# A mixture-of-experts kernel: tables moved to GpSimd, weight pieces twice as wide, norm sums placed inside a step

## What is computed

```python
def _gemma_mlp(x, gate_w, up_w, down_w):
    g = jnp.einsum('bsh,hi->bsi', x, gate_w)          # 128 -> 512
    u = jnp.einsum('bsh,hi->bsi', x, up_w)
    return jnp.einsum('bsi,ih->bsh', gelu(g) * u, down_w)

rw = jax.nn.softmax(router_logits, axis=-1)           # (32, 8)
w, sel = jax.lax.top_k(rw, 2); w = w / w.sum(axis=-1, keepdims=True)
w = scale * w + (1.0 - scale) * stop_gradient(w)      # scale = 1/12
out = sum over experts e of dense_w[:, e] * _gemma_mlp(x, skill_gate[e], skill_up[e], skill_down[e])
out = out + _gemma_mlp(x, shared_gate, shared_up, shared_down)
return x + out
```

## Time and profile before

| | us |
|---|---|
| median of 3 runs | 214.37 (213.44 to 215.72) |
| the profiled execution, its own time | 213.45 |
| its span on the core | 211.6 |
| TensorE busy | 202.7 |
| ScalarE busy | 137.6 |
| VectorE busy | 127.8 |
| GpSimd busy | 107.9 |

### The profile page before, as it was taken

One profiled execution on the slowest core, in us unless ns is written; L12 is line 12 of the kernel. 1 busy time (PEld: TensorE's weight loads), 2 busy tenths in 40 slices (PEclk: granted clock), 3 DMA queues, 4 the chain that ended last, 5 costly groups with the idle time before them and its releaser, 6 DMA issues.

```text
span 211.6 us, 6607 instructions
## 1 busy us (share of the span) xinstructions
PE 202.7 (96%) x2663; PEld 162.8 (77%) x2663; DVE 127.8 (60%) x231; ACT 137.6 (65%) x225; POOL 107.9 (51%) x110
## 2 busy tenths in 40 slices
PE   7999597999989999999999999999999999999995
PEld 2345353544434468899999999999999999999995
DVE  4796986788889999754434434435435344444451
ACT  6356377799997999656556566565565665655650
POOL 3002324446544666765655656556556556565562
PEclk9999999999999999999999999999999999999999
DMA  6999600000000000000010010010010010010011
GB/s 203 402 427 437 268 3 0 2 3 0 0 0 0 0 3 5 0 5 3 3 50 3 3 52 4 0 53 3 5 51 5 0 53 3 5 50 3 3 53 53
DMA packets 2814, 11.70 MB, mean 55 GB/s; under 512 B 353, under 2 KB 609, under 8 KB 2401
## 3 DMA queue, kind: packets, MB, share of 16 engines
q1 hardware_dynamic: 2640, 11.01, 13.0%
q10 hardware_dynamic: 144, 0.26, 0.5%
HBM read 9.18 MB, written 2.10 MB: 53 GB/s over the span
## 4 chain that ended last, share of the span: by engine, by line
PE 68%; ACT 11%; DVE 3%; issue 1%; DVEq 0%
PE o_ps L670 7%; PE u_ps L650 7%; PE g_ps L650 7%; PE o_ps L668 7%; PE u_ps L652 7%; PE g_ps L652 7%; PE o_ps L669 7%; PE u_ps L651 7%; PE g_ps L651 7%; ACT gel L298 3%; ACT wsk L320 3%; ACT h L303 3%; ACT wsk L315 1%; PE o_ps L631 1%; PE o_ps L632 1%; PE o_ps L633 1%
## 5 line engine op out<-in xcount | busy, mean ns | idle before, releaser
L271 POOL TENSOR_TENSOR h<-h 128x512 f16<-128x512 f32 x92 | 106.1, 1159 | 99.2 <-ACT h L303 68.8
L453 DVE SCALAR_TENSOR_TENSOR h<-gel,sk_factor,u_ps 128x512 f32<-128x512 f32 x64 | 47.8, 747 | 66.5 <-PE u_ps L652 35.3
L298 ACT ACTIVATE gel<-g_ps,sk_gate 128x512 f32<-128x512 f32 x64 | 44.0, 687 | 48.8 <-PE g_ps L652 48.8
L303 ACT CAST h<-h 128x512 f16<-128x512 f32 x92 | 56.4, 613 | 4.9 <-DVE h L453 4.6
L652 PE MATMUL g_ps<-x,wsk 128*128 128x128 f16 x256 | 46.2, 219 | 0.0
L652 PE MATMUL u_ps<-x,wsk 128*128 128x128 f16 x256 | 46.2, 219 | 0.0
L651 PE MATMUL g_ps<-x,wsk 128*128 128x128 f16 x256 | 46.2, 219 | 0.0
L651 PE MATMUL u_ps<-x,wsk 128*128 128x128 f16 x256 | 46.2, 219 | 0.0
L650 PE MATMUL g_ps<-x,wsk 128*128 128x128 f16 x256 | 46.1, 219 | 0.0
L650 PE MATMUL u_ps<-x,wsk 128*128 128x128 f16 x256 | 46.1, 219 | 0.0
L670 PE MATMUL o_ps<-h,wsk 128*128 128x128 f16 x256 | 45.9, 219 | 0.0
(11 more groups left out here) (107 smaller groups left out, 307.2 us busy)
## 6 DMA issues: line engine op xcount, KB each, us to landing
wsk<-skills SPq DMA_DIRECT2D x3, 2048.0 KB, 16.5
outT<-xT SPq DMA_DIRECT2D x7, 256.0 KB, 2.0
xT<-xT SPq DMA_DIRECT2D x2, 768.0 KB, 6.8
wsh<-shared SPq DMA_DIRECT2D x3, 256.0 KB, 3.8
xT<-xT ACTq DMA_DIRECT2D x1, 256.0 KB, 3.4
xT<-xT SPq DMA_DIRECT2D x1, 256.0 KB, 5.2
outT<-xT SPq DMA_DIRECT2D x1, 192.0 KB, 2.8
outT<-xT SPq DMA_DIRECT2D x1, 64.0 KB, 1.6
```

The source lines that it names most:

```text
L271: nc.gpsimd.tensor_tensor(hidden_lo(t), hidden_full(t), hidden_hi(t), ALU.subtract).then_inc(lo_ok, 1)
L298: nc.scalar.activation(gel[:, t % NG, :], g_ps[t % 2][:, :], ACT.Gelu_apprx_tanh, scale=scale).then_inc(gelu_ok, 1)
L303: nc.scalar.copy(hidden_hi(t), hidden_full(t)).then_inc(hi_ok, 1)
L453: nc.vector.scalar_tensor_tensor(out=h32[:, t % N32, :], in0=gel[:, t % NG, :], scalar=factor, in1=u_ps[t % 2][:, :], op0=ALU.mult, op1=AL ...
```

## The change

**Front.** The first four steps take group 0 of x instead of group 7, and the groups follow in their order. ScalarE fetches group 0 and behind it, on the same queue, the router logits, which SyncE fetched first of all before; SyncE so starts with the shared weights. The set FIRST holds x of groups 0 and 1 (`XF = 2`), X_NEXT groups 2 to 4, X_REST groups 5 to 7. `routing_weights` and `routing_spread` move from the front and from step 4 to VectorE's step 3.

**Order.** The maxima of groups 5, 6, 7 move to steps 10, 11, 11, the mask and the sum of X_REST to steps 12 and 13; `routed_tables` from 7 to 11; `add_group(0)` from 10 to 7. The splits of x move to one or two steps earlier relative to their use; that of group 0, needed by the experts only, is new at step 3. On TensorE `spread_norms` stands between d and u of its step rather than behind u. On VectorE `scales` stands ahead of `mask`.

**Tables.** All factor tables are made by GpSimd, between its `hidden_lo`: FIRST ahead of the steps, X_NEXT in step 4, X_REST in step 14, the experts' in step 22. VectorE waits for them where it uses a new one.

**Experts' weights.** The down matrix gets its norm by `gram` on TensorE in steps 15 to 18; ScalarE's `squares` are gone. The experts' weights are split in 6 pieces of 2048 columns, at steps 12, 16, 20, 24, 28 and 32, instead of 12 of 1024 every other step from 12 to 34.

```diff
-        TOP_AT = {1: (1,), 3: (2, 3), 5: (4, 5), 6: (6, 7)}
-        K_STEPS = [5, 9]
-        MASK_AT = {3: X_NEXT, 6: X_REST, 8: K_GATE, 12: K_UP, 22: K_DOWN}
-        SPREAD_AT = {4: X_NEXT, 7: X_REST, 9: K_GATE, 13: K_UP, 23: K_DOWN}
-        SQUARES_AT = {11: 0, 13: 1, 17: 2, 21: 3}
+        TOP_AT = {1: (2,), 3: (3, 4), 10: (5,), 11: (6, 7)}
+        K_STEPS = [5, 10, 15]
+        MASK_AT = {3: X_NEXT, 9: K_GATE, 12: X_REST, 14: K_UP, 19: K_DOWN}
+        SPREAD_AT = {4: X_NEXT, 10: K_GATE, 13: X_REST, 15: K_UP, 20: K_DOWN}
         ROUTE_AT = 6
+        ROUTED_AT = 11
+        TABLE_AT = {4: X_NEXT, 14: X_REST}
+        SKILL_TABLES_AT = 22
-        X_AT = {5: 1, 8: 7, 9: 2, 10: 3, 15: 4, 19: 5, 23: 6}
-        EG = 2
-        PIECES = {12 + 2 * n: n for n in range(3 * E // EG)}
+        X_AT = {3: 0, 5: 2, 8: 3, 10: 4, 14: 5, 18: 6, 22: 7}
+        EG = 4
+        PIECES = {12 + 4 * n: n for n in range(3 * E // EG)}
...
         def _(sp):
-            sp.dma_start(logits[:, :], cond).then_inc(cond_in, 16)
...
         def _(act):
-            act.dma_start(xT32[:, (G - 1) * GN:], xT[:, (G - 1) * GN:]).then_inc(x_in[0], 16)
+            act.dma_start(xT32[:, 0:GN], xT[:, 0:GN]).then_inc(x_in[0], 16)
+            act.dma_start(logits[:, :], cond).then_inc(cond_in, 16)
...
             probabilities()
-            routing_weights()
             for q in (GATE, UP, DOWN):
                 top_shared(q)
             top_x(0)
+            top_x(1)
             mask(FIRST)
...
-                if t in MASK_AT:
-                    mask(MASK_AT[t])
                 if t in SPREAD_AT:
-                    n = SPREAD_AT[t]
-                    scales(n)
-                    if n == X_NEXT:
-                        shared_tables(1, XA, 2)
-                    if n == X_REST:
-                        shared_tables(XA, G, 3)
-                        inverse_table()
-                if t == C:
+                    scales(SPREAD_AT[t])
+                if t in MASK_AT:
+                    mask(MASK_AT[t])
+                if t == C - 1:
+                    routing_weights()
                     routing_spread()
-                if t == ROUTE_AT + 1:
+                if t == ROUTED_AT:
                     routed_tables()
-                if t == 24:
-                    skill_tables()
-
-                if t == 10:
+
+                if t == 7:
                     add_group(0)
...
                     if down_of(t) >= C and down_of(t) != down_of(t - 1):
                         down_shared(down_of(t))
+                    if t in SPREAD_AT:
+                        spread_norms(SPREAD_AT[t])
                     half_shared(t, UP)
...
-                if t in SPREAD_AT:
-                    spread_norms(SPREAD_AT[t])
...
-                for kind in range(2):
+                for kind in range(3):
                     n = t - K_STEPS[kind]
                     if 0 <= n < 4:
...
                 if t in PIECES:
                     pool.wait_ge(sk_lo_ok, PIECES[t] + 1)
                 nc.gpsimd.tensor_tensor(hidden_lo(t), hidden_full(t), hidden_hi(t), ALU.subtract).then_inc(lo_ok, 1)
+                if t in TABLE_AT:
+                    shared_tables(TABLE_AT[t])
+                if t == SKILL_TABLES_AT:
+                    skill_tables()
```

More of the change, by code:

```diff
@@ L46, in build @@
     N32 = 4
+    XF, XA = 2, 5
     NG = 3
@@ L169, in build @@
         stored = sem("stored")
[L174 to L176 removed]
+        FIRST, X_NEXT, K_GATE, X_REST, K_UP, K_DOWN = range(6)
+        K_OF = (K_GATE, K_UP, K_DOWN)
+        COLS = [(DC, XC + XF), (XC + XF, XC + XA), (KC, KC + 1), (XC + XA, XC + G), (KC + 1, KC + 2), (KC + 2, KC + 3)]
         def group(t):
[L181 to L196 removed]
+            return t // C
+        TOP_AT = {1: (2,), 3: (3, 4), 10: (5,), 11: (6, 7)}
+        TOP_OF = {FIRST: 3 + XF, X_NEXT: 3 + XA, X_REST: 3 + G}
+        K_STEPS = [5, 10, 15]
+        MASK_AT = {3: X_NEXT, 9: K_GATE, 12: X_REST, 14: K_UP, 19: K_DOWN}
+        SPREAD_AT = {4: X_NEXT, 10: K_GATE, 13: X_REST, 15: K_UP, 20: K_DOWN}
+        ROUTE_AT = 6
+        ROUTED_AT = 11
+        TABLE_AT = {4: X_NEXT, 14: X_REST}
+        SKILL_TABLES_AT = 22
+        X_AT = {3: 0, 5: 2, 8: 3, 10: 4, 14: 5, 18: 6, 22: 7}
+        X_NTH = {1: 1} | {j: n + 2 for n, j in enumerate(X_AT.values())}
+        EG = 4
+        PIECES = {12 + 4 * n: n for n in range(3 * E // EG)}
         def lag(t):
@@ L305, in x_high @@
             def x_high(j):
-                act.wait_ge(scaled, (FIRST if j == 0 else X_NEXT if j < XA else X_REST) + 1)
+                act.wait_ge(scaled, (FIRST if j < XF else X_NEXT if j < XA else X_REST) + 1)
                 nc.scalar.activation(x_part(j, 0), x_full(j), ACT.Copy, scale=sc[:, XC + j:XC + j + 1]).then_inc(x_hi_ok, 1)
[L309 to L315, removed]
             def skill_high(n):
                 kind, w, hi, _ = piece_of(n)
-                act.wait_ge(scaled, K_GATE + kind + 1)
+                act.wait_ge(scaled, K_OF[kind] + 1)
                 nc.scalar.activation(hi, w, ACT.Copy, scale=sc[:, KC + kind:KC + kind + 1]).then_inc(sk_hi_ok, 1)
@@ L363, in mask @@
                 a, b = COLS[n]
-                if n < K_GATE:
+                if n not in K_OF:
                     dve.wait_ge(top_ok, TOP_OF[n])
                     nc.vector.tensor_tensor(top2[:, a:b], top[:, a:b], top[:, a:b], ALU.mult).then_inc(diag_ok, 1)
[L367 to L370, removed]
-                else:
-                    dve.wait_ge(sq_ok, E // 2)
-                    nc.vector.tensor_scalar(sq_floor[:, :], sq_sum[:, :], NORM_FLOOR, None, ALU.add).then_inc(diag_ok, 1)
+                else:
+                    kind = K_OF.index(n)
+                    dve.wait_ge(gram_ok, kind + 1)
+                    nc.vector.scalar_tensor_tensor(out=diag[:, :], in0=n_ps[0][:, 0:P], scalar=NORM_FLOOR,
+                                                   in1=ident[:, :], op0=ALU.add, op1=ALU.mult).then_inc(diag_ok, 1)
             def scales(n):
@@ L378, in scales @@
                 norm = n_ps[1][:, 0:b - a]
-                if n >= K_GATE:
+                if n in K_OF:
                     norm = n_all[:, a:b]
-                    nc.vector.tensor_reduce(norm, n_ps[1][:, 0:E // 2 if n == K_DOWN else P], AX.X, ALU.max).then_inc(n_red, 1)
-                    dve.wait_ge(n_red, n - K_GATE + 1)
+                    nc.vector.tensor_reduce(norm, n_ps[1][:, 0:P], AX.X, ALU.max).then_inc(n_red, 1)
+                    dve.wait_ge(n_red, K_OF.index(n) + 1)
                 nc.vector.tensor_scalar(e_bits[:, a:b], norm.bitcast(U32), 1, EXP_MASK,
@@ L423, in skill_tables @@
[L423 to L433, removed]
-                nc.vector.scalar_tensor_tensor(out=sk_inv[:, :], in0=tmp_k[:, 0, :], scalar=inv[:, KC + 2:KC + 3],
-                                               in1=sk_gate[:, :], op0=ALU.mult, op1=ALU.mult).then_inc(tab_sk, 1)
-                dve.wait_ge(tab_sk, 1)
@@ L530, in _ @@
                     scales(FIRST)
-                    shared_tables(0, 1, 1)
                 if t in TOP_AT:
@@ L709, in _ @@
                             pe.wait_ge(sk_in[kind], 16)
-                        if n == 0 and kind == UP:
-                            pe.wait_ge(diag_ok, K_GATE + 1)
+                        if n == 0 and kind:
+                            pe.wait_ge(diag_ok, K_OF[kind - 1] + 1)
                         a = (kind * E + 2 * n) * I
                         for half in range(2):
-                            last = gram(n_ps[0][:, 0:P], wsk32[:, a + half * I:a + (half + 1) * I], n == 0 and half == 0)
+                            last = gram(n_ps[0][:, 0:P], wsk32[:, a + half * I:a + (half + 1) * I],
+                                        n == 0 and half == 0)
                         if n == 3:
```

80 lines of the change are left out of this document (49 added, 31 removed).

## The result

The changed kernel takes 219.31 us (219.19 to 219.63, 4 runs) against 213.91: ratio 1.023, 95% interval 1.017 to 1.029. The profiled execution took 219.63, its span is 217.8, 6.2 above the span before. The interval is wide because the kernel before itself varies, here from 213.37 to 215.72; the last experiment shows most of the reason.

A forecast was written before the change was run, and what follows sets the result against it. TensorE was taken to bound the kernel. Front +0.6, gram +1.9, removed waits -5.6 and new waits +6.3 gave +3.2 on the profiled 213.45; with the median 0.9 higher, 217.6 us, range 212.6 to 219.8 (forecast's own 216.3 to 218.8).

The forecast's parts named there:

- three signs of being wrong: Second L589 (X_REST's sum) waits under 1.0 us; logits come near 2.8; late waits exceed 2.
- The front: Before the shared steps: logits queued behind group 0 of x make the sum of FIRST later, +0.6 us (-0.4 to +1.1).
- gram: TensorE's norm of the down matrix: four portions of 0.47 add 1.9 us.
- waits removed: Shared steps: all five TensorE waits of the kernel before can go, -5.6 us.
- K_GATE: Step 10: TensorE's sum waits 0.6 us for its mask, behind a hidden value and the low part of x group 3.
- X_REST: Step 13: TensorE's sum waits 2.0 us (1.5 to 2.5) for its mask; VectorE needs 5.5 against TensorE's 3.5.
- K_DOWN: Step 20: TensorE's sum waits 1.1 us for its mask, with the low part of x group 6 ahead.
- step 8: TensorE's d there is late by up to 0.6 us because step 5's low part waits for x group 2; booked 0.4.
- K_UP: Step 15: mask behind a 2048-column low part; wait 0.9 us, or 1.9 if the scales meet GpSimd; taken 1.4.
- Late steps: Steps 24 to 36: 2048-column pieces make hidden values late, 0.8 us (0.2 to 2.0), including 1.0 once if one meets GpSimd.
- Rival 1: VectorE keeps each mask ahead of TensorE's sums, so the new waits vanish: 211.3 us; chance 0.17.
- Rival 3: Wide pieces hold up the late steps, ScalarE at 2.3 and VectorE meeting GpSimd at each piece: 220.5 us; chance 0.08.

The follow-up runs named there:

- experiment 12: The last one: the kernel before, unchanged, run again with a profile; full-clock executions took 213.01 and 213.91 us, the six at clock 0.992 took 215.20 to 216.02.
- experiment 1: Changed kernel with the router logits issued first on SyncE's queue, ahead of the shared weights; 218.27 us.
- experiment 2: Changed kernel with the logits still on ScalarE's queue but issued ahead of group 0 of x; 218.26 us.
- experiment 6: Changed kernel with the down matrix's norm made by ScalarE's four squares (steps 9, 11, 15, 17) instead of gram; 219.26 us.
- experiment 11: Kernel of experiment 10 with the down matrix's norm by ScalarE's squares in steps 11, 12, 16, 20 instead of gram; 210.39 us, ratio 0.977 to the kernel before.
- experiment 8: Changed kernel with the experts' tables in GpSimd's step 24 instead of step 22; 219.33 us.
- experiment 9: Changed kernel with logits first on ScalarE's queue, sums behind u, and masks, routed_tables, gram, experts' tables and group 0's split moved; wide pieces kept; 214.54 us.
- experiment 7: Changed kernel with all factor tables made by VectorE right behind their scales instead of by GpSimd, the experts' in step 24; 221.98 us.
- experiment 5: Changed kernel with the experts' weights split in 12 pieces of 1024 columns, every other step from 12 to 34; 217.58 us.
- experiment 4: Changed kernel with the four routed_tables instructions in VectorE's step 8 instead of step 11; 218.09 us.
- experiment 10: Changed kernel with logits first on ScalarE's queue, sums behind u, masks and tables moved, 1024-column pieces every other step from 13; 211.55 us, ratio 0.985 to the kernel before.

## Why the prediction came out as it did

Forecast 217.6, measured 219.31, in the range of 212.6 to 219.8 but above the forecast's own 216.3 to 218.8; slower was the likeliest outcome, and the mechanism is the one forecast. The number flatters the sum. The profiled execution grew by 6.2, nearly twice the +3.2 forecast and at the upper bound of +6.1. The median came nearer because it was taken 0.9 above the profiled execution before and lay 0.3 below the one after; that is luck. None of the three signs of being wrong came: the second sum waited 1.99, `neg_max` started at 5.49, the late waits stayed under 2. Step by step:

- *What bounds it.* Right. The experts' part is 133.2 (132.7), the float32 stretch 7.00 both times, so each delay went into the time.
- *The front, +0.6.* Right in kind, mis-sized: 1.54, outside my upper bound of 1.1. The term that failed is "I take the logits at 4.35" (bound 4.8): they landed at 5.45, 1.1 later. I had let them land with x or with the first weights; both were themselves later (4.2 and 4.0 from issue instead of 3.4 and 3.6 to 4.0), and the logits came after both. Experiments 1 and 2 show the cause. Part of the size is chance: against the second profile of the kernel before (sum of FIRST at 9.46) the front costs 0.94, while the changed kernel has this sum at 10.17 to 10.43 in all seven profiles with its front.
- *gram, waits removed.* The sizes are right, 1.9 and 5.6. But experiment 6 shows that gram's 1.9 was not worth 1.9: without it the next mask keeps TensorE just as long. In a chain of waits, terms do not add that way.
- *K_GATE, X_REST, K_DOWN, step 8.* 0.63, 2.15, 1.04, 0.56 against 0.6, 2.0, 1.1, 0.4. The order in VectorE's queue, laid out instruction by instruction against TensorE's, gave them. The cast took 0.73 rather than 1.16 (I took 0.66).
- *K_UP.* 1.9, my upper value: the scales did meet GpSimd. I took the middle of two outcomes, of which one had to come.
- *Late steps, 0.8.* Measured 1.84, near my upper bound of 2.0. The 1.0 that I allowed "once" came, at the place and for the reason named; beside it stood four of 0.16 to 0.22. The bound had allowed for this, the 0.8 had not. This item is short by 1.0, the front by 0.9, K_UP by 0.5: 2.4 of the 3.0 by which the sum was short; the rest is 0.15 each at X_REST and step 8 and the 0.2 named under the table. All new waits together are 8.2, where the forecast had 6.3 (3.8 to 8.7).
- *Rival 1* (VectorE keeps ahead) would have needed the 5.5 us from step 11 on to fit 3.5; they took 5.6. *Rival 3* (220.5) is nearer to 219.31 than the forecast is, but its conditions did not hold: ScalarE's piece took 2.00, not 2.3, and one of VectorE's six pieces met GpSimd (3.28), the other five took 2.35.
- Not foreseen: the half clock. In the profiled execution it lies under K_UP's wait and costs nothing; in the kernel before it costs 1.7 us in the trace, and some 2 between the two groups of executions, so it narrows the difference between the kernels.

## What to carry to other kernels

Cost a moved instruction by what stands behind it in its own queue and by how much work the waiting engine still has, not by the engine's mean load: here less work on both helpers (VectorE and ScalarE) came with 5.4 us more. A sum that waits for a mask belongs as late in TensorE's step as its user allows, and a long piece never ahead of a mask. Where a chain of such waits is present, taking work off the bounding engine gives nothing until the next wait is gone (experiments 6 and 11), and moving one collision can only move it on (experiment 8).

## What the runs showed of the hardware

- A 1 KB transfer behind a 256 KB one on the same queue took 4.3 us to land; first on ScalarE's queue it took 2.5 and started its user at 3.27, first on SyncE's 1.7 and 2.46.
- A VectorE instruction of three columns beside a GpSimd instruction of 1.16 took 1.14 instead of 0.16, a 2048-column piece 3.3 instead of 2.35, and a cast of eight numbers 0.16 (experiment 9, GpSimd idle), 0.73 or 1.16. Instructions of one column (0.14 at 34.91, when GpSimd was idle, and at 63.85 in the kernel before, when it was not) showed no such delay.
- TensorE's granted clock fell to half for 3.4 us, 0.6 to 1.3 us after it took up work from 2 to 3.5 us of idling, in five of the profiles (the kernel before in experiment 12, the changed one, experiments 1, 6 and 7). After the same 2.15 us of idling it stayed full in experiments 2, 5 and 8, at X_REST's sum in experiment 7 and in the first profile of the kernel before. What decides between the two stays open. The kernels of experiments 4, 10 and 11, whose longest wait is 1.93, 0.57 and 1.04, had the full clock in every execution.
